# Layer norm rows and the betas' sigmoid on ScalarE, page counts in two VectorE operations

## The reference, cut to what matters

```python
def _layernorm(x, axis=-1, eps=1e-05):
    m = jnp.mean(x, axis=axis, keepdims=True)
    v = jnp.var(x, axis=axis, keepdims=True)
    return (x - m) / jnp.sqrt(v + eps)

# attention: 16 heads of 64, two states S and R per head, one step per position
xn = (x - mu) / jnp.sqrt(var + LN_EPS) * ln_w + ln_b
q, k, v = xn @ Wq.T, xn @ Wk.T, xn @ Wv.T
alpha, aR = sigmoid(xn @ Wa.T + ba), sigmoid(xn @ WaR.T + baR)
beta, gamma = sigmoid(xn @ Wb.T + bb), sigmoid(xn @ Wg.T + bg)
# step: kn = k / |k|;  r = clip(v - S'kn, -1, 1)
#       S = a*S;  S += b * kn (v - kn S)';   o = S'q
#       R = aR*R; R += g * kn (r - kn R)';   o += R'q
out = os @ Wo.T + residual

# ffn: 64 experts, the best 8 of a position by a grouped sigmoid router, plus one shared expert
h = silu(x @ Wg[e]) * (x @ Wu[e]) * coef[e];  moe_out = sum over e of h @ Wd[e]
return moe_out + silu(x @ SWg) * (x @ SWu) @ SWd
```

## Time and profile before

| | |
|---|---|
| median of three runs | 3295.07 us (3291.97 to 3296.05) |
| the profiled execution | 3276.76 us, span 3274.9 us |
| busy in the span: PE, DVE, ACT, POOL | 85%, 83%, 59%, 29% |
| granted TensorE clock, mean of the span | 0.906 |
| the 32 passes of the loop | the first begins at 75.4 us, the last at 2466.2 us, so 77.1 us apart |

### The profile page before, as it was taken

The page is one execution under the profiler, slowest core; times in us unless marked ns, Lnnn a source line. Parts: engine busy times, 40 slices in busy tenths (PEclk is TensorE's granted clock), DMA queues, the critical chain, the costliest instruction groups (busy, mean ns, idle before and its releaser), DMA issues. The chain is left out here.

```text
span 3274.9 us, 132532 instructions
## 1 busy us (share of the span) xinstructions
PE 2773.5 (85%) x55642; PEld 2460.6 (75%) x55642; DVE 2721.3 (83%) x6827; ACT 1943.8 (59%) x5180; POOL 953.5 (29%) x928
## 2 busy tenths in 40 slices
PE   3888888888888888888888888888886199999986
PEld 3878888887787888788788888888786177777664
DVE  2889898888989988999999999999997156777776
ACT  2656555556666655666666555666654077666664
POOL 3112222222222222223222222233221101444444
PEclk8988898888888988989999899999998599999998
DMA  3321111111111111111111111111110945777776
GB/s 116 82 64 37 36 35 35 35 35 37 39 35 35 37 37 35 43 35 35 39 40 41 35 35 35 35 42 35 39 40 30 347 144 170 221 217 224 220 217 180
DMA packets 209563, 264.55 MB, mean 81 GB/s; under 512 B 30673, under 2 KB 183250, under 8 KB 208210
## 3 DMA queue, kind: packets, MB, share of 16 engines
q1 hardware_dynamic: 183936, 188.53, 19.0%
q0 software_dynamic: 24576, 67.27, 7.2%
q10 hardware_dynamic: 466, 0.27, 0.0%
HBM read 125.37 MB, written 130.58 MB: 78 GB/s over the span
## 5 line engine op out<-in xcount | busy, mean ns | idle before, releaser
L379 POOL DMA_INDIRECT table<-tail,places x256 | 277.1, 1082 | 721.1 <-DVE BR L852 214.8
L1496 PE MATMUL bank<-w,tail 128*128 x1280 | 357.2, 401 | 31.4 <-ACT tail L1539 14.5
L1468 POOL DMA_INDIRECT tail<-y_table,places x256 | 249.5, 975 | 449.3 <-DMA y_table<-tail 314.0
L1091 POOL COPY inv_r<-N 32x512 f32<-32x512 f32 x128 | 136.4, 1065 | 734.0 <-DVE N L827 730.0
L445 DVE TENSOR_TENSOR tri<-tri,step 128x58 f32<-128x58 f32 (+13 forms) x896 | 305.5, 341 | 30.8
L444 DVE TENSOR_TENSOR step<-tri 128x58 f32<-128x58 f32 (+13 forms) x896 | 301.4, 336 | 26.4
L1496 PEld LDWEIGHTS bank<-w,tail 128*128 128x128 f32 x1280 | 219.2, 191 | 95.9 <-issue 72.7
L1586 DVE TENSOR_TENSOR more<-tail 128x1 f32<-128x1 f32 x320 | 50.8, 159 | 193.7 <-ACT tail L1548 189.6
L1511 PE MATMUL bank<-w,tail 128*128 x640 | 191.1, 380 | 2.7 <-DVE tail L1597 1.4
L1546 ACT ACTIVATE tail<-bank 128x129 f32<-128x129 f32 x320 | 89.8, 281 | 158.9 <-PE bank L1496 156.3
L1482 PE MATMUL bank<-ident,tail 128*128 128x128 f32 x640 | 125.1, 278 | 66.1 <-DMA tail<-table 65.6
(11 more groups left out here) (275 smaller groups left out, 8103.8 us busy)
## 6 DMA issues: line engine op xcount, KB each, us to landing
table<-blank SPq DMA_DIRECT2D x320, 128.5 KB, 3.2
tail<-table SPq DMA_DIRECT2D x320, 128.5 KB
y_table<-tail SPq DMA_DIRECT2D x320, 128.0 KB
w<-in_wpack_dram SPq DMA_DIRECT2D x16, 1540.0 KB, 19.3
tail<-in_x_dram SPq DMA_DIRECT2D x66, 64.0 KB, 2.5
x_rows<-tail SPq DMA_DIRECT2D x32, 128.0 KB
sh_rows<-tail SPq DMA_DIRECT2D x32, 128.0 KB, 1.9
table<-tail,places POOLq DMA_INDIRECT x256, 2.9
```

What stands on the lines that cost most here:

```text
L379: nc.gpsimd.indirect_dma_start(out=table, out_offset=bass.IndirectOffsetOnAxis(ap=t.places[:, TOP * (n - 1) + k:TOP * (n - 1) + k + 1], ax ...
L1468: nc.gpsimd.indirect_dma_start(out=t.term[2 * (m % 2) + k], out_offset=None, in_=d.y_table[0:P * closed(b) + P + 1, :], in_offset=bass.Ind ...
L1496: mm = nc.tensor.matmul(ps[:, 0:257], t.xT_slot[i % 3][:, P * kt:P * kt + P], weights(i, 257 * kt, 257), start=(kt == 0), stop=(kt == 1))
```

## The change

All four layer norms of a pass are now written by ScalarE. `ln_apply` is gone from VectorE, and `ln_guess` on ScalarE has become `layer_norm`: it negates the mean (an activation Copy with scale -1), makes 1/sqrt as before, multiplies the two (a Copy whose scale is a value per partition), and writes the 256 columns by an Identity whose bias and scale are values per partition. VectorE waits for `y_normed` before it adds the residual. The sigmoid of the betas, which VectorE ended by an addition and a reciprocal, is ended by a Ln and an Exp on ScalarE. `count_pages` compares with three columns in one operation and adds in a second, where it was three operations that did both.

```diff
-def count_pages(nc, t, n):
-    for i in range(3):
-        ins = nc.vector.scalar_tensor_tensor(out=t.page_seen[:, i, :], in0=t.pages[n % 2][:], scalar=t.tile_of[:, i:i + 1],
-                                             in1=t.page_seen[:, i, :], op0=ALU.is_le, op1=ALU.add)
-    return ins
+def count_pages(nc, t, n, link):
+    link(nc.vector.tensor_tensor(t.page_hit[:], over(t.pages[n % 2][:], 3), bc(t.tile_of[:], E), ALU.is_le))
+    return nc.vector.tensor_tensor(t.page_seen[:], t.page_seen[:], t.page_hit[:], ALU.add)
...
@@ vector
-            def ln_apply(i, order, dst, src):
-                dve.wait_ge(t.sem["ln_guess_ready"], order)
-                dve.wait_ge(t.sem["ln_var_ready"], order)
-                return nc.vector.tensor_scalar(dst, src, t.mv[:, i, 0:1], t.ln_tmp[:, i, 1:2],
-                                               ALU.subtract, ALU.mult)
...
-                link(ln_apply(2, norms + 1, t.y[:, :], t.y[:, :]))
+                dve.wait_ge(t.sem["y_normed"], n + 1)
...
-                ln_apply(3, norms + 2, t.xrow[n % 2][:, 0:256], t.y[:, :]).then_inc(t.sem["xf_ready"], 1)
...
-                    ln_apply(0, norms + 3, res[:, :], t.x_new[:, :]).then_inc(t.sem["res_ready"], 1)
...
-                    link(nc.vector.tensor_scalar(beta[:], t.bgz[:], 1.0, None, ALU.add))
-                    nc.vector.reciprocal(beta[:], beta[:]).then_inc(t.sem["beta_ready"], 1)
...
-                    ln_apply(1, norms + 4, t.xhat[:, :], t.res[(n + 2) % 3][:, :]).then_inc(t.sem["xhat_ready"], 1)
@@ scalar
-            def ln_guess(i, order):
+            def layer_norm(i, order, dst, src):
+                tmp = t.ln_tmp[:, i, :]
                 act.wait_ge(t.sem["ln_var_ready"], order)
-                link(nc.scalar.activation(t.ln_tmp[:, i, 0:1], t.mv[:, i, 1:2], ACT.Ln, bias=t.tiny[:, 2:3]))
-                nc.scalar.activation(t.ln_tmp[:, i, 1:2], t.ln_tmp[:, i, 0:1], ACT.Exp,
-                                     scale=-0.5).then_inc(t.sem["ln_guess_ready"], 1)
+                nc.scalar.activation(tmp[:, 0:1], t.mv[:, i, 0:1], ACT.Copy, scale=-1.0)
+                link(nc.scalar.activation(tmp[:, 1:2], t.mv[:, i, 1:2], ACT.Ln, bias=t.tiny[:, 2:3]))
+                link(nc.scalar.activation(tmp[:, 1:2], tmp[:, 1:2], ACT.Exp, scale=-0.5))
+                link(nc.scalar.activation(tmp[:, 0:1], tmp[:, 0:1], ACT.Copy, scale=tmp[:, 1:2]))
+                return nc.scalar.activation(dst, src, ACT.Identity, bias=tmp[:, 0:1], scale=tmp[:, 1:2])
...
-                ln_guess(2, norms + 1)
+                layer_norm(2, norms + 1, t.y[:, :], t.y[:, :]).then_inc(t.sem["y_normed"], 1)
...
-                ln_guess(3, norms + 2)
+                layer_norm(3, norms + 2, t.xrow[n % 2][:, 0:256], t.y[:, :]).then_inc(t.sem["xf_ready"], 1)
                 if ahead:
-                    ln_guess(0, norms + 3)
+                    layer_norm(0, norms + 3, t.res[(n + 2) % 3][:, :], t.x_new[:, :]).then_inc(t.sem["res_ready"], 1)
...
                     gate_exp(nc, t, mm(n, "BG")).then_inc(t.sem["front_act"], 1)
+                    wait_emptied(act, t, o, n, "BG")
+                    link(nc.scalar.activation(t.bgz[:], t.bgz[:], ACT.Ln, bias=1.0))
+                    nc.scalar.activation(t.beta[(n + 1) % 2][:], t.bgz[:], ACT.Exp, scale=-1.0).then_inc(t.sem["beta_ready"], 1)
...
-                    ln_guess(1, norms + 4)
+                    layer_norm(1, norms + 4, t.xhat[:, :], t.res[(n + 2) % 3][:, :]).then_inc(t.sem["xhat_ready"], 1)
```

More of the change, by code:

```diff
@@ L162, in alloc_shared @@
              "mm_done", "front_mm", "dve_emptied", "act_emptied", "out_emptied", "front_dve", "front_act",
-             "dve_link", "act_link", "ln_var_ready", "ln_guess_ready", "xhat_ready", "x2_made", "res_ready",
+             "dve_link", "act_link", "ln_var_ready", "ln_guess_ready", "xhat_ready", "x2_made", "y_normed", "res_ready",
              "keys_squared", "norm_ready", "bg_exp_ready", "beta_ready", "key_ready",
@@ L205, in alloc_tail @@
     t.page_seen = take(3 * E).rearrange("p (k n) -> p k n", n=E)
+    t.page_hit = take(3 * E).rearrange("p (k n) -> p k n", n=E)
     t.tile_of, t.page_order = take(3), take(3)
@@ L773, in _ @@
                 front, route, ahead = flags(n)
-                norms = o.base("ln_var_ready", n)
                 dve.wait_ge(t.sem["act_diag"], 2 * n + 2)
@@ L790, in _ @@
                 invert_steps(nc, t, link, 7, 11)
-                if n >= 2:
-                    wait_done(dve, t, o, n - 2, "RT")
-                ln_apply(3, norms + 2, t.xrow[n % 2][:, 0:256], t.y[:, :]).then_inc(t.sem["xf_ready"], 1)
                 wait_emptied(dve, t, o, n - 1, "V1")
@@ L812, in _ @@
                                             ALU.mult).then_inc(t.sem["dve_emptied"], 1)
-                if front:
-                    wait_emptied(dve, t, o, n, "BG")
-                    beta = t.beta[(n + 1) % 2]
-                    link(nc.vector.tensor_scalar(beta[:], t.bgz[:], 1.0, None, ALU.add))
-                    nc.vector.reciprocal(beta[:], beta[:]).then_inc(t.sem["beta_ready"], 1)
                 invert_steps(nc, t, link, 15, 20)
-                if ahead:
-                    wait_done(dve, t, o, n, "XT")
-                    ln_apply(1, norms + 4, t.xhat[:, :], t.res[(n + 2) % 3][:, :]).then_inc(t.sem["xhat_ready"], 1)
                 for h in range(2):
@@ L891, in _ @@
                     route_record(nc, t, link, n)
-                    count_pages(nc, t, n)
+                    count_pages(nc, t, n, link)
                 wait_emptied(dve, t, o, n, "OUT")
@@ L981, in _ @@
                     exp_gate(n, 1)
-                    need(act, t, "beta_ready", n)
                     gate_exp(nc, t, mm(n, "BG")).then_inc(t.sem["front_act"], 1)
+                    wait_emptied(act, t, o, n, "BG")
+                    link(nc.scalar.activation(t.bgz[:], t.bgz[:], ACT.Ln, bias=1.0))
+                    nc.scalar.activation(t.beta[(n + 1) % 2][:], t.bgz[:], ACT.Exp, scale=-1.0).then_inc(t.sem["beta_ready"], 1)
                     log_gate(n, 0)
@@ L1339, in _ @@
             route_record(nc, t, link, chunks)
-            link(count_pages(nc, t, chunks))
+            link(count_pages(nc, t, chunks, link))
             link(nc.vector.tensor_reduce(t.page_order[:], t.page_seen[:], AX_X, ALU.add))
```

## The result

The changed kernel takes 3358.3 us (median of four runs, 3355.71 to 3360.39) where the kernel before took 3295.56 (3291.97 to 3303.34): the ratio is 1.0187, with a 95% interval of 1.0166 to 1.0207, so 55 to 68 us slower. The forecast was +46 and 3341. The profiled execution took 3356.27 us, span 3354.5.

What follows compares the result with a forecast made beforehand. VectorE and the TensorE–ScalarE chain were taken to bound the kernel jointly, meeting at `N`. Delays of 44.4 us, 2.2 for pages and small end terms gave +46.5, so 3295 + 46 = 3341 us; range 3320 to 3370 (8 in 10).

Steps and rivals of the forecast that it cites:

- What bounds the kernel: Whole pass: VectorE and the TensorE–ScalarE chain arrive together at `N` (33.88 us); VectorE waits at two places, `BR` and `k`.
- The wait at `pqT`: VectorE before PQ's results: its saving of 1.21 us there becomes a new wait of about 2 us a pass.
- What arrives on ScalarE: ScalarE: each layer norm costs 1.48 us, 1.05 more than a guess; bounds 1.20 and 1.85.
- the page count: VectorE just before zero: two operations take 0.66 us against 0.59, a loss of 0.07 us a pass.
- First and second delay: Pass start: `xnT` moves from 0.53 to 1.58 us; exponentials of `a` from 5.98 to 7.53, 1.55 later.
- The sign that I named: Start of a pass: TensorE's idle time before `a` grows by 1 us in the changed profile.
- the first delay lies inside this one: TensorE before `r0`: `a` and KR end at 7.36 us, so the exponentials set `r0` at 8.71.
- the clock takes more: Rival: longer TensorE idle lowers the clock, PQ slow in 18 more passes, 30 us more, 3371; chance 0.13.
- gives it back: Rival: shifted work keeps the clock up behind `N` in 20 passes, 48 us back, 3293; chance 0.05.
- N and the join at the copies of the inverse: Middle of a pass: `N` some 1.05 us late, ScalarE 1.55 late and last; everything behind moves by 1.55.
- The sum: Whole kernel: 44.4 us for 30 passes, 2.2 for pages, +0.7 and −0.8 for two passes; together +46.5 us.
- VectorE's saving has no value: VectorE, each pass: the 1.95 us it saves is nowhere on the path.

Runs made afterwards that it cites:

- norm 0 behind the gate: Changed kernel with ScalarE's layer norm 0 moved behind the first gate's exponentials; ratio 1.0204 to the kernel before.
- `xnT` first: Changed kernel with the two copies that make `xnT` moved ahead of layer norm 2 on ScalarE; ratio 1.0245 to the kernel before.
- second profile of before: The kernel before, unchanged, timed and profiled once more on chip 15; ratio 0.9989, loop 2384.4 us.
- norms alone: All four layer norms on ScalarE, betas' sigmoid and page count as in the kernel before; ratio 1.0189 to the kernel before.
- betas and pages alone: Kernel before with only the betas' sigmoid on ScalarE and pages counted by two operations, layer norms as before; ratio 0.9969.
- split kernel: Kernel before with norms 0 and 1 written in ScalarE's idle time, betas' sigmoid on ScalarE, norms 2 and 3 as before; ratio 0.9905, 3239.2 us.
- `xnT` and gate first: Changed kernel with `xnT` copies ahead of layer norm 2 and first gate's exponentials ahead of norms 3 and 0; ratio 0.9995 to the kernel before.
- the control: Kernel before with `xnT` ahead of guess 2 and first gate's exponentials ahead of guesses 3 and 0, nothing moved between engines; ratio 1.0006.

## Why the prediction was right in size, and where its working was not

*What bounds the kernel.* Right, but for a third place at which VectorE waited, `L_s`, 13.3 us in all. VectorE's 91% was not the whole bound, and the 48 us that it gave up became waits at `pqT` and `rqT`, with as much again for the longer loop. The wait at `pqT` is 3.8 us a pass, where I had written about 2.

*What arrives on ScalarE, and the page count.* Right to the hundredth. A layer norm was put at 1.48 and is 1.49, the page count at 0.66 and is 0.66; the two operations that had no row in the trace of before are these (count | busy, mean ns):

```profile
L903 ACT ACTIVATE tail<-tail 128x256 f32<-128x256 f32 x64 | 38.4, 600 | 2.1
L902 ACT ACTIVATE tail<-tail 128x1 f32<-128x1 f32 x124 | 36.5, 294 | 4.0
```

By the figures of the Trainium skill, "ScalarE: Activation LUTs", section "What ACT_TABLE_LOAD costs", the Identity is 585 ns and a norm 1.46 us, both an estimate. The trace agrees within 3%.

*First and second delay.* `xnT` at 1.58 and exponentials at 7.52 were forecast as 1.58 and 7.53. The sign that I named, TensorE's idle time before `a` up by 1 us, is not in the two profiles as they stand (1.61 us in both passes shown) and appears like with like: 12.8 and 43.5 us in all on one kind of chip, 1.6 and 2.7 us a time on the other. What failed is the step between them: "the first delay lies inside this one, since `a` and KR end at 6.31 + 1.05 = 7.36". They end at 8.8 (by the mean 9.1), because `a` runs at the low clock in 25 of 26 passes, where it did in 3 of 26 and 0 of 26 in the two profiles of before. r0 came at 8.75, close to my 8.71, but by another road, and that the two roads are of one length is luck. The run with norm 0 behind the gate shows it, and the run with `xnT` first shows that the second delay would have done it too.

*The clock.* I gave "the clock takes more" 0.13 as a rival with a fixed sum; it is part of nearly every pass. TensorE spent 17.3 us a pass (4th to 30th) at the low level against 14.3 and 13.5, and PQ ran at it in 18 of 26 passes against 4 and 6. It moved as well: in the first 8 us of a pass from at most 0.4 to 3.9 us, around PQ (16 to 20 us) from 0.3 to 2.1, and just behind `N`'s old place (36 to 40 us) from 3.3 down to 0.5. So both rivals of the clock, "takes more" and "gives it back", came true in part, at different places of a pass. The Trainium skill, "TensorE: Matmul & The Clock Gate", section "Part 1: The HAM clock gate (the "warmup" mystery)", says that activity releases the low level and its absence brings it back; the falls behind the longer waits at `a` and `r` agree in direction.

*N and the join at the copies of the inverse.* Forecast: `N` 1.05 late, ScalarE 1.55 late. Measured: 2.8 and 3.2 by the median, 2.4 and 2.75 by the mean (some passes of before had a slow PQ and a late `N` too). ScalarE was the last, as said. What the forecast lacks is the clock: PQ ended 3.2 us late and not 1.55, and in the two passes in which it ended at 18.9, near my 18.75, `N` was at 35.2, near my 34.9. Behind the copies part of it came back. By the mean the 2.75 at the copies are 2.3 at `BR`, 2.1 at `k` and 2.0 at the next zero, against my 1.55 at all of them. A pass is 2.0 us longer by this mean, 1.6 by the median and by the loop over all 31, against my 1.48 + 0.07.

*The sum.* The loop grew by 48 us where I had 46.5; against the second profile of before it is 55. The timed difference is 63. That 48 stands beside 46.5 is in part luck, for two terms that I had at nothing, the loss by the clock up to PQ and what came back behind the copies, largely cancel. The rest of the 63, 8 to 15 us, lies outside the loop or in the difference between one profiled execution and the median of many; the runs with the norms alone have executions from 3351 to 3389 us. I have no run that settles it.

*VectorE's saving has no value.* Too strong, by what the runs suggest. The betas and pages alone brought 3 to 18 us, the split kernel more than TensorE's 0.5 us a pass, and with `xnT` and gate first `N` comes 1.3 us earlier where PQ runs at full speed. Where ScalarE is not made late, VectorE's saving seems to count. No run takes work from VectorE and does nothing else, so its price is not shown.

## What to carry to other kernels

Ask of work that is moved to an engine with idle time not how full the engine is but which of its instructions the next one waits for, and put the new work behind that one: the same instructions cost 63 us in one order and nothing in another, and part of them, placed in idle time, gained 31. If TensorE's wait before a block of products grows, as here by a microsecond, look at the granted clock in the products behind it before you blame the next wait. When two delays each suffice, removing one shows nothing; remove both. Compare profiles by the stretch that the edit touches, and from the same chip, for the rest may differ by more than the effect. And do not subtract medians of places along a pass to say where time was won: take the mean as well.

## What the runs showed of the hardware that was not expected

About a microsecond more or less of idle time decided which clock `a` got. With a single idle time of 1.6 us ahead of it, 3 of 26 passes (before) and 0 of 26 (split) had `a` at the 1.2 GHz level. With one of 2.7 us (norm 0 behind the gate), or with one of 0.4 and one of 1.6 and the rest of `S`'s products between them (the changed kernel), it was 25 of 26, and the products took 5.6 us in the mean against 3.84. An idle time of 4.1 us ahead of `r` did the same there in all 26 (5.47 us). In the control, which waits at neither, both ran at full speed in all 26.

A part of the program with the same code and data took 628 to 636 us on one chip and 655 to 667 on another, and the same 64 small products of a pass had a pause of some 0.4 us on the second in nearly every pass (24 to 26 of 26) and on the first in none.
